# Expert rows that carry gate, token number and residual, answered by a scatter to the output

## The chip, the cores and the metric

The kernel runs on one core of a Trainium2 chip. The metric is the device time of one execution in microseconds (us), the median of several runs. Its engines are PE (TensorE, matrix products), DVE (VectorE), ACT (ScalarE), POOL (GpSimd) and SP (SyncE, which here only issues transfers). They run side by side and meet at semaphores. SBUF is the on-chip memory of 128 partitions, PSUM the accumulator memory of eight banks.

## What is computed

Two layers on four images of 1024 tokens with 64 features. The change touches only the last part, the layer of eight experts with a capacity:

```python
C = max(1, math.ceil(CAPACITY_FACTOR * T / E))          # 1.25 * 4096 / 8 = 640
logits = x @ gate_w + gate_b
probs = jax.nn.softmax(logits, axis=-1)
idx = jnp.argmax(probs, axis=-1)
prb = jnp.take_along_axis(probs, idx[:, None], axis=1)[:, 0]
one_hot = jax.nn.one_hot(idx, E, dtype=jnp.float32)
pos = (jnp.cumsum(one_hot, axis=0) * one_hot).sum(-1).astype(jnp.int32) - 1
kept = pos < C
buf = jnp.zeros((E, C, D)).at[idx, pos_safe].set(x, mode='drop')
hmid = jax.nn.relu(jnp.einsum('ecd,edf->ecf', buf, w1) + b1[:, None, :])
ybuf = jnp.einsum('ecf,efd->ecd', hmid, w2) + b2[:, None, :]
y_tok = ybuf[idx, jnp.minimum(pos, C - 1)] * (prb * kept)[:, None]
y = jnp.nan_to_num(y_tok, nan=0.0, posinf=10000.0, neginf=-10000.0)
out = h + y                                             # x above is layernorm(h)
```

T is 4096 tokens, D is 64, the hidden width is 256. Every token goes to one expert, each expert takes at most 640 tokens, and 8 x 640 = 5120 slots exist for 4096 tokens.

## The kernel before

The program is a row of stages with a barrier of all engines behind each: setup, a loop over the four images (tokens, project, windowed), then experts (first layer), full (second attention), batchnorm and routed. Within a stage each engine has its own list of instructions, in the order in which they are written, and waits only where the code waits on a semaphore. There is no scheduler; what stands in the list of an engine behind a wait is held by it.

The stage routed is the one that changes. Tokens lie as 32 tiles of 128 (ALLT). It runs like this:

- DVE normalises all tokens (L1241 to L1250), PE turns them and forms the gate logits (L1162, L1171), ACT takes the exponential (L1225), DVE picks the expert, PE counts tokens per expert (L1176, L1177), DVE computes the slot of every token and from it two lists of row numbers: `send_to` (L1293) and `fetch_from` (L1299).
- POOL sends each of the 32 tiles with one indirect transfer, 128 rows of 64 floats, to the DRAM buffer `sent_rows` at the rows of `send_to` (L1342). Tokens over the capacity go to spare rows behind the 5120.
- SP waits for all 32 and loads the 5120 rows back in five pieces of 256 KB (L1356). PE turns them in 20 transposes of two tokens side by side, 128 by 128 (L1183), so that one half of the rows of the PE array holds one token's features and the other half the other's. ACT and DVE copy the turned tiles out (L1228, L1305).
- The experts follow one after the other: `hidden` (L1196), two products of 320 columns for each of two halves of the hidden width, one on array rows 0 to 63 and one on rows 64 to 127; ReLU on ACT (L1235) and on DVE (L1318); `outputs` (L1207), five tiles with two products each; the second bias on DVE (L1310). SP stores each expert's answers to the DRAM buffer `answered_rows` (L1360).
- When all eight are stored, POOL gathers for each of the 32 token tiles its 128 answer rows (L1347). For every group of four tiles DVE multiplies by the gate, replaces not-a-number and infinities and adds the residual `res` (L1326 to L1335, eight groups of nine instructions), and SP writes the group to the output (L1363).

`sent_rows` is filled with zeros in the stage batchnorm, by eight transfers on SP (L1088) that SP waits for at the end of that stage.

## Time and profile before

| | |
|---|---|
| median of 3 runs | 1095.16 us (1093.58 to 1095.29) |
| profiled execution: its time | 1091.47 us |
| profiled execution: its span | 1089.6 us |
| stage routed, from its first DVE instruction to the end of the span | 922.5 to 1089.6 us |
| PE, DVE, ACT, POOL busy, share of the span | 68, 57, 41, 34% |
| granted PE clock, mean over the span | 0.837 |

The span is what the trace covers; 1.9 us of the profiled execution's time lie outside of it. Shares of busy time are means over stages with different limits. The change is confined to the last sixth of the span, and there PE, DVE and POOL take turns, which the means don't show.

### The profile page before, as it was taken

The page shows a single profiled execution, that of the slowest core. Times are in us where ns is not written, and L with a number is a line of the kernel's source. Part 1 is how long each engine was busy: PE and PEld are TensorE (multiplying, and loading weights), DVE is VectorE, ACT ScalarE, POOL GpSimd, SP SyncE. Part 2 cuts the span into 40 slices and gives each one's busy share as a digit, 9 for nine tenths or more (in the row PEclk, how much of TensorE's full clock was granted, in tenths as well). Part 3 has the DMA queues.
Part 4 walks back from the last instruction along what each step waited for, and adds up shares of the span by engine and source line. Part 5 has one row for each costly group of instructions (what it writes and reads, how often), then busy time and mean ns, then how long its engine had stood idle before and what let it go on. Part 6 is the DMA issues. An engine that isn't in the chain of part 4 may idle for free. (4 is left out here: it accounts for less than half of the span.)

```text
span 1089.6 us, 21917 instructions
## 1 busy us (share of the span) xinstructions
...
## 2 busy tenths in 40 slices
...
DMA packets 51471, 43.60 MB, mean 40 GB/s; under 512 B 46484, under 2 KB 47956, under 8 KB 50452
## 3 DMA queue, kind: packets, MB, share of 16 engines
...
q0 software_dynamic: 2048, 2.10, 0.8%
q8 instruction: 75, 1.23, 0.5%
q14 instruction: 30, 0.25, 0.1%
...
## 5 line engine op out<-in xcount | busy, mean ns | idle before, releaser
L721 ACT ACTIVATE work<-ps,small,rq 128x160 f32<-128x160 f32 x512 | 243.0, 486 | 51.3 <-DVE small L674 51.1
L700 POOL TENSOR_TENSOR work<-work,small 128x512 f32<-128x512 f32 x128 | 133.1, 1040 | 144.9 <-DVE small L688 144.9
L671 DVE TENSOR_REDUCE ps<-ps 128x4 f32<-128x640 f32 x128 | 106.5, 832 | 60.2 <-PE ps L607 60.2
L682 DVE COPY pT<-ps 128x640 f32<-128x640 f32 x128 | 105.4, 823 | 8.3 <-PE ps L620 7.9
L607 PE MATMUL ps<-kT,big 64*128 64x160 f32 x1024 | 107.1, 333 | 0.0
L721 ACT ACTIVATION_READ_ACCUMULATOR work<-ps,small,rq 128x1 f32 x512 | 104.9, 205 | 0.0
L1342 POOL DMA_INDIRECT sent_rows<-big,xb x32 | 30.8, 964 | 202.2 <-DVEq L1294 192.8
L262 PE MATMUL ps<-xT,s_proj_w 64*128 64x512 f32 x288 | 82.7, 701 | 18.3 <-DVE xb L545 11.7
L572 POOL TENSOR_TENSOR big<-xb 128x1024 f32<-128x1024 f32 x32 | 75.1, 2358 | 55.0 <-DVE xb L545 54.9
L637 PE MATMUL ps<-pT,vwin 128*64 128x128 f32 x1024 | 85.1, 284 | 10.2 <-ACT big L709 2.4
L607 PEld LDWEIGHTS ps<-kT,big 64*128 64x128 f32 x1024 | 83.9, 208 | 0.4
L495 ACT ACTIVATE big<-ps 128x1024 f32<-128x1024 f32 x32 | 32.8, 1023 | 96.3 <-DVE xb L545 96.3
L637 PEld LDWEIGHTS ps<-pT,vwin 128*64 128x64 f32 x1024 | 57.4, 137 | 24.2 <-issue 16.0
L1006 PE MATMUL ps<-xb,big 64*128 64x64 f32 x1024 | 65.2, 277 | 0.9 <-DVE hl L1070 0.9
L1006 PEld LDWEIGHTS ps<-xb,big 64*128 64x128 f32 x1024 | 62.5, 193 | 1.0 <-issue 1.0
L262 PEld LDWEIGHTS ps<-xT,s_proj_w 64*128 64x128 f32 x288 | 30.4, 219 | 64.5 <-issue 38.0
L620 PE MATMUL ps<-s_ident,work 64*128 64x64 f32 x1024 | 56.7, 230 | 2.4 <-DVE pT L682 2.4
L603 PE MATMUL ps<-window_mask,row_of_t 64*128 64x128 bf16 (+1 forms) x256 | 33.1, 254 | 37.0 <-PEq L208 25.0
L634 PE MATMUL ps<-pT,vrem 32*64 32x128 f32 x1024 | 57.7, 295 | 0.0
L709 ACT ACTIVATE big<-ps 128x256 f32<-128x256 f32 x128 | 48.5, 379 | 16.4 <-PE ps L634 16.2
L565 POOL MEMSET vwin<- 128x256 f32 x4 | 1.2, 311 | 159.2 <-POOLq L208 159.2
L1038 ACT ACTIVATE big<-ps,h 128x1024 f32<-128x1024 f32 x32 | 35.6, 1113 | 42.2 <-DVE h L1059 42.2
...
## 6 DMA issues: line engine op xcount, KB each, us to landing
...
```

What stands on the lines that cost most here:

```text
L262: ins = nc.tensor.matmul(bank[banks + w][:], proj_w[half_rows(w), cols], xT[half_rows(w), :], start=True, stop=True)
L572: g.tensor_tensor(dst, first, second, ALU.add).then_inc(S["rot_done"], 1)
L607: ins = nc.tensor.matmul(tiles[e][:, hh, :], qT[half_rows(e), c, 4 * hh:4 * hh + 4, :].rearrange("p a t -> p (a t)"), kT[half_rows(e), CHU ...
L620: ins = nc.tensor.transpose(bank[4 + r][:, D * q:D * q + D], src, ident[half_rows(r), half_rows(r)])
L634: ins = nc.tensor.matmul(o, vrem[r, c, :], pT[r, c % 2, NQ * P:], start=False, stop=True, tile_position=(CHUNK * q, D * e), skip_group_che ...
L637: nc.tensor.matmul(o, vwin[:, c, :], pT[:, c % 2, P * q:P * q + P], start=True, stop=True, skip_group_check=True)
L671: ch.step(v.tensor_reduce(row_max(c), ps[:, s_banks(c), 0:2 * SPAN].rearrange("p e (h k) -> p e h k", h=2), X, ALU.max))
L682: v.tensor_copy(pT[:, c % 2, :].rearrange("p (q r t) -> p r q t", r=2, t=D), ps[:, 4:6, 0:(NQ + 1) * D].rearrange("p r (q t) -> p r q t", ...
L700: g.tensor_tensor(probs[:, c % 3, :, 0:P], probs[:, c % 3, :, 0:P], bc(small[:, c % 4, 3, :], P), ALU.mult)
L709: nc.scalar.activation(oT[:, :, CHUNK * c:CHUNK * (c + 1)].rearrange("p (h a) t -> p h a t", h=2), ps[:, 6:8, 0:P].rearrange("p h (a t) -> ...
L721: nc.scalar.activation(probs[:, c % 3, q, :], bank[2 * (c % 2) + e][:, SPAN * hh:SPAN * hh + SPAN], ACT.Exp, bias=small[:, c % 4, 1, q:q + ...
L1006: ins = nc.tensor.matmul(bank[6 + r][:, 0:D], pT1[half_rows(r), i % 2, P * k:P * k + P], v1[half_rows(r), TILES * (i // TILES) + k, :], st ...
```

## The change

- Each sent row grows from 64 to 130 floats (ROW, 520 bytes): the normalised token, its residual `res`, its gate and its token number as an integer. ACT copies the normalised tokens and the residual into the array `payload` (after's L1234, L1235), DVE writes the other two columns. POOL's sends now also wait for ACT's copies.
- The row of a slot in `sent_rows` is chosen so that the 40 tiles that come back (SLOT_TILES) each hold 128 slots of one expert. `fetch_from`, its four DVE instructions and the array of gates go.
- The empty rows of `sent_rows` are now written in the stage full, from `empty_row`, whose last two floats are 1.0; read as an integer that is a token number far past 4095.
- SP writes `res` to the whole output at the start of routed, one transfer of 1 MB.
- The rows come back in five pieces of 532 KB, eight tiles each. PE turns the five tiles of one expert at a time (`turn_back`, 40 transposes in all), one expert ahead of its products. ACT copies three of the five turned tiles and DVE two (`keep_back`). The turned tiles occupy 64 partitions, so both products of `hidden` use array rows 0 to 63. `hidden` uses two pairs of banks in turn instead of three.
- `answer(e)` on DVE adds the bias and then does the whole end of the computation for one expert's five tiles: gate, replacement of special values, residual. The store to `answered_rows`, the gather and the output transfers of the groups go.
- POOL scatters each of the expert's five tiles straight to the output at the token numbers that came along (40 transfers); row numbers past 4095 are left out by `bounds_check`.

The core of the diff; declarations and unchanged layouts are left out:

```diff
+COPIED_BY_ACT = 3 * P
+GATE_AT, TOKEN_AT, ROW = 2 * D, 2 * D + 1, 2 * D + 2
...
+                v.memset(empty_row[:, 0:TOKEN_AT], 0.0)
+                v.memset(empty_row[:, TOKEN_AT:], 1.0)
...
+            @block.sync
+            def _(sp):
+                for k in range(E):
+                    sp.dma_start(sent_rows[CAPACITY * k:CAPACITY * (k + 1), :].rearrange("(p t) d -> p t d", p=P),
+                                 empty_row[:].unsqueeze(1).to_broadcast([P, CAPACITY // P, ROW])).then_inc(S["zero_done"], 16)
+                sp.wait_ge(S["zero_done"], 16 * E)
...
-                for k in range(E):
-                    sp.dma_start(sent_rows[CAPACITY * k:CAPACITY * (k + 1), :].rearrange("(p t) d -> p t d", p=P),
-                                 zeros[:, 0:D].unsqueeze(1).to_broadcast([P, CAPACITY // P, D])).then_inc(S["zero_done"], 16)
                 sp.wait_ge(S["x_loaded"], 16 * 5)
-                sp.wait_ge(S["zero_done"], 16 * E)
...
         def both(n):
-            return ps[:, 2 * (n % 3):2 * (n % 3) + 2, 0:CAPACITY // 2].rearrange("p a (t s) -> p a t s", s=SLOT_ROWS)
+            return ps[:, 2 * (n % 2):2 * (n % 2) + 2, 0:CAPACITY // 2]
...
-                for t in range(HALF_TILES):
-                    if t % 4 == 0:
-                        pe.wait_ge(S[f"back{t // 4}"], 16)
-                    ins = nc.tensor.transpose(bank[t // 4][:, P * (t % 4):P * (t % 4) + P], came[:, t, :], ident[:])
-                    if t % 4 == 3:
-                        ins.then_inc(S["turned_back"], 1)
+                def turn_back(e):
+                    pe.wait_ge(S[f"back{(PER_EXPERT * e + PER_EXPERT - 1) // 8}"], 16)
+                    if e >= 1:
+                        pe.wait_ge(S["low_done"], e)
+                        pe.wait_ge(S["xT_dve"], e)
+                    for j in range(PER_EXPERT):
+                        b, col = divmod(P * j, COPIED_BY_ACT)
+                        ins = nc.tensor.transpose(bank[4 + b][0:D, col:col + P], came[:, PER_EXPERT * e + j, 0:D], ident[:])
+                    ins.then_inc(S["turned_back"], 1)
 
                 def hidden(n):
-                    e, f = divmod(n, 2)
-                    if n < 3:
-                        pe.wait_ge(S["xT_dve"], (HALF_TILES // 4) // 2)
-                        pe.wait_ge(S["low_done"], HALF_TILES // 4 - (HALF_TILES // 4) // 2)
-                    else:
-                        pe.wait_ge(S["hid_dve" if (n - 3) % 2 else "hid_act"], (n - 3) // 2 + 1)
-                    for a in range(2):
-                        r = slice(D * a, D * a + D)
-                        ins = nc.tensor.matmul(bank[2 * (n % 3) + a][:, 0:CAPACITY // 2], ffn_w[r, P * n:P * n + P],
-                                               came_turned[r, :, SLOT_ROWS * e:SLOT_ROWS * (e + 1)], start=True, stop=True)
+                    e = n // 2
+                    pe.wait_ge(S["low_done"], e + 1)
+                    pe.wait_ge(S["xT_dve"], e + 1)
+                    if n >= 2:
+                        pe.wait_ge(S["hid_dve" if n % 2 else "hid_act"], n // 2)
+                    for w in range(2):
+                        ins = nc.tensor.matmul(bank[2 * (n % 2) + w][:, 0:CAPACITY // 2], ffn_w[0:D, P * n:P * n + P],
+                                               came_turned[:, e % 2, CAPACITY // 2 * w:CAPACITY // 2 * (w + 1)],
+                                               start=True, stop=True)
                     ins.then_inc(S["proj_done"], 1)
 
...
+                turn_back(0)
                 for e in range(E + 1):
+                    if e + 1 < E:
+                        turn_back(e + 1)
                     if e < E:
                         hidden(2 * e)
                         hidden(2 * e + 1)
...
-                for k in range(0, HALF_TILES // 4, 2):
-                    a.wait_ge(S["turned_back"], k + 1)
-                    nc.scalar.activation(came_turned[:, 4 * k:4 * k + 4, :].rearrange("p j n -> p (j n)"), bank[k][:],
+                nc.scalar.activation(xn_sent, xn_all[:], ACT.Copy).then_inc(S["rest_done"], 1)
+                nc.scalar.activation(res_sent, res[:], ACT.Copy).then_inc(S["rest_done"], 1)
+
+                def keep_back(e):
+                    a.wait_ge(S["turned_back"], e + 1)
+                    if e >= 2:
+                        a.wait_ge(S["proj_done"], 2 * (e - 1))
+                    nc.scalar.activation(came_turned[:, e % 2, 0:COPIED_BY_ACT], bank[4][0:D, 0:COPIED_BY_ACT],
                                          ACT.Copy).then_inc(S["low_done"], 1)
...
+                v.tensor_copy(payload[:, :, GATE_AT], sa[3])
+                v.tensor_scalar(payload[:, :, TOKEN_AT].bitcast(I32), spare_rows, float(-E * CAPACITY), None, ALU.add)
...
-                for k in range(1, HALF_TILES // 4, 2):
-                    v.wait_ge(S["turned_back"], k + 1)
-                    v.tensor_copy(came_turned[:, 4 * k:4 * k + 4, :].rearrange("p j n -> p (j n)"),
-                                  bank[k][:]).then_inc(S["xT_dve"], 1)
+
+                def keep_back(e):
+                    v.wait_ge(S["turned_back"], e + 1)
+                    if e >= 2:
+                        v.wait_ge(S["proj_done"], 2 * (e - 1))
+                    v.tensor_copy(came_turned[:, e % 2, COPIED_BY_ACT:], bank[5][0:D, 0:CAPACITY - COPIED_BY_ACT]).then_inc(
+                        S["xT_dve"], 1)
+
+                keep_back(0)
...
                 def answer(e):
+                    tiles = slice(PER_EXPERT * e, PER_EXPERT * e + PER_EXPERT)
+                    by_tile = y_gated.rearrange("p (j d) -> p j d", d=D)
                     v.wait_ge(S["y_psum"], e + 1)
-                    v.tensor_tensor(answers[:, e], bank[6 + e % 2][:, 0:PER_EXPERT * D].rearrange("p (j d) -> p j d", d=D),
-                                    rows(ffn_b2[:, e, :], PER_EXPERT), ALU.add).then_inc(S["y_ready"], 1)
...
-                for gg in range(GROUPS):
-                    v.wait_ge(S[f"got{gg}"], 16 * G)
-                    at = slice(gg * G, gg * G + G)
-                    ch.step(v.tensor_tensor(y_gated.rearrange("p (i d) -> p i d", d=D), fetched[:, at, :],
-                                            bc(gates[:, at], D), ALU.mult))
+                    ins = v.tensor_tensor(by_tile, bank[6 + e % 2][:, 0:PER_EXPERT * D].rearrange("p (j d) -> p j d", d=D),
+                                          rows(ffn_b2[:, e, :], PER_EXPERT), ALU.add)
+                    ch.step(ins)
+                    v.sem_inc(S["y_ready"], 1)
+                    ch.step(v.tensor_tensor(by_tile, by_tile, bc(came[:, tiles, GATE_AT], D), ALU.mult))
                     v.memset(y_finite, 0.0)
                     ch.step(v.tensor_tensor(maski, y_gated, y_gated, ALU.is_equal))
                     ch.step(v.copy_predicated(y_finite, maski, y_gated))
...
-                    v.tensor_tensor(y_out[:, gg, :], y_finite, res[:, at, :].rearrange("p i d -> p (i d)"),
+                    v.tensor_tensor(answers[:, e].rearrange("p (j d) -> p j d", d=D),
+                                    y_finite.rearrange("p (j d) -> p j d", d=D), came[:, tiles, D:2 * D],
                                     ALU.add).then_inc(S["last"], 1)
+
+                for e in range(E):
+                    if e + 1 < E:
+                        keep_back(e + 1)
+                    n = 2 * e + 1
+                    v.wait_ge(S["proj_done"], n + 1)
+                    if e >= 2:
+                        v.wait_ge(S["y_psum"], e - 1)
+                    v.tensor_scalar(hid[:, e % 2, 1].rearrange("p (w n) -> p w n", w=2), both(n), ffn_b1[:, n:n + 1], 0.0,
+                                    ALU.add, ALU.max).then_inc(S["hid_dve"], 1)
+                    if e:
+                        answer(e - 1)
+                answer(E - 1)
...
                 g.wait_ge(S["slots_ready"], 1)
+                g.wait_ge(S["rest_done"], 2)
                 for i in range(ALLT):
                     g.indirect_dma_start(sent_rows, bass.IndirectOffsetOnAxis(send_to[:, i:i + 1].bitcast(U32), 0),
-                                         xn_all[:, i, :], None).then_inc(S["sent"], 16)
-                g.wait_ge(S["slots_ready"], 2)
-                g.wait_ge(S["stored"], 16 * E)
-                for i in range(ALLT):
-                    g.indirect_dma_start(fetched[:, i, :], None, answered_rows,
-                                         bass.IndirectOffsetOnAxis(fetch_from[:, i:i + 1].bitcast(U32), 0)).then_inc(
-                                             S[f"got{i // G}"], 16)
+                                         payload[:, i, :], None).then_inc(S["sent"], 16)
+                g.wait_ge(S["stored"], 16)
+                for e in range(E):
+                    g.wait_ge(S["last"], e + 1)
+                    for j in range(PER_EXPERT):
+                        g.indirect_dma_start(out_rows, bass.IndirectOffsetOnAxis(
+                            came[:, PER_EXPERT * e + j, TOKEN_AT:TOKEN_AT + 1].bitcast(U32), 0),
+                            answers[:, e, D * j:D * j + D], None, bounds_check=IMAGES * SEQ - 1,
+                            oob_is_err=False).then_inc(S["zero_done"], 16)
 
             @block.sync
+                sp.dma_start(out, res[:]).then_inc(S["stored"], 16)
                 sp.wait_ge(S["sent"], 16 * ALLT)
-                back = sent_rows[0:E * CAPACITY, :].rearrange("(p t h) d -> p t (h d)", h=2, t=HALF_TILES)
+                back = sent_rows[0:E * CAPACITY, :].rearrange("(p t) d -> p t d", t=SLOT_TILES)
                 for k in range(CHUNKS_X):
-                    sp.dma_start(came[:, 4 * k:4 * k + 4, :], back[:, 4 * k:4 * k + 4, :]).then_inc(S[f"back{k}"], 16)
-                store = answered_rows.rearrange("(p e j) d -> p e j d", e=E, j=PER_EXPERT)
-                for e in range(E):
-                    sp.wait_ge(S["y_ready"], e + 1)
-                    sp.dma_start(store[:, e], answers[:, e]).then_inc(S["stored"], 16)
-                for gg in range(GROUPS):
-                    sp.wait_ge(S["last"], gg + 1)
-                    sp.dma_start(out[:, gg * G:gg * G + G, :], y_out[:, gg, :].rearrange(
-                        "p (i d) -> p i d", d=D)).then_inc(S["x_loaded"], 16)
-                sp.wait_ge(S["x_loaded"], 16 * GROUPS)
+                    sp.dma_start(came[:, 8 * k:8 * k + 8, :], back[:, 8 * k:8 * k + 8, :]).then_inc(S[f"back{k}"], 16)
+                sp.wait_ge(S["stored"], 16)
+                sp.wait_ge(S["zero_done"], 16 * SLOT_TILES)
```

PE's list for one expert in the middle of the loop, before. `big` is the turned rows or the hidden values, `xb` the weights:

```order
L1196 MATMUL ps<-big,xb 128x320 [waits hid_dve]
L1196 MATMUL ps<-big,xb 128x320
L1196 MATMUL ps<-big,xb 128x320 [waits hid_act]
L1196 MATMUL ps<-big,xb 128x320
L1207 MATMUL ps<-xb,big 128x64 [waits y_ready,hid_dve,hid_act]
L1207 MATMUL ps<-xb,big 128x64 x9
```

The same place in the changed kernel, L1190 being `turn_back`, L1200 `hidden` and L1212 `outputs`:

```order
L1190 MATMUL ps<-s_ident,big 64x128 [waits xT_dve,low_done,back3]
L1190 MATMUL ps<-s_ident,big 64x128 x4
L1200 MATMUL ps<-big,xb 128x320 [waits hid_act,xT_dve,low_done]
L1200 MATMUL ps<-big,xb 128x320
L1200 MATMUL ps<-big,xb 128x320 [waits hid_dve,xT_dve,low_done]
L1200 MATMUL ps<-big,xb 128x320
L1212 MATMUL ps<-xb,big 128x64 [waits y_ready,hid_dve,hid_act]
L1212 MATMUL ps<-xb,big 128x64 x9
```

Five transposes of the next expert's tiles have moved into the loop ahead of each expert's products, with waits on the arriving rows and on the copies of the expert before.

DVE's list, before, at the end of the expert loop and the first group of the gathered rows:

```order
L1318 TENSOR_SCALAR big<-ps,xb 128x2x20x16 [waits y_psum,proj_done]
L1310 TENSOR_TENSOR big<-ps,xb 128x320 [waits y_psum] x2
L1326 TENSOR_TENSOR vwin<-big,xb 128x256 [waits got0]
L1328 MEMSET vwin 128x256 [waits dve_chain]
L1329 TENSOR_TENSOR vwin<-vwin 128x256
L1330 COPY_PREDICATED vwin<-vwin 128x256 [waits dve_chain]
L1331 TENSOR_SCALAR vwin<-vwin 128x256 [waits dve_chain]
L1332 COPY_PREDICATED vwin<-vwin,xb 128x256 [waits dve_chain]
L1333 TENSOR_SCALAR vwin<-vwin 128x256 [waits dve_chain]
L1334 COPY_PREDICATED vwin<-vwin,xb 128x256 [waits dve_chain]
L1335 TENSOR_TENSOR vrem<-vwin,res 128x256 [waits dve_chain]
```

The changed kernel's DVE list for one expert in the middle of the loop: the copy of turned tiles, the ReLU, then `answer`:

```order
L1318 COPY big<-ps 64x256 [waits proj_done,turned_back]
L1350 TENSOR_SCALAR big<-ps,xb 128x640 [waits y_psum,proj_done]
L1327 TENSOR_TENSOR vwin<-ps,xb 128x320 [waits y_psum]
L1331 TENSOR_TENSOR vwin<-vwin,big 128x320 [waits dve_chain]
L1332 MEMSET vwin 128x320 [waits dve_chain]
L1333 TENSOR_TENSOR vwin<-vwin 128x320
L1334 COPY_PREDICATED vwin<-vwin 128x320 [waits dve_chain]
L1335 TENSOR_SCALAR vwin<-vwin 128x320 [waits dve_chain]
L1336 COPY_PREDICATED vwin<-vwin,xb 128x320 [waits dve_chain]
L1337 TENSOR_SCALAR vwin<-vwin 128x320 [waits dve_chain]
L1338 COPY_PREDICATED vwin<-vwin,xb 128x320 [waits dve_chain]
L1339 TENSOR_TENSOR big<-vwin,big 128x320 [waits dve_chain]
```

The nine instructions of a group stood behind the gather; now they stand inside every step of the expert loop, on 320 columns instead of 256.

POOL's list of the stage, before:

```order
L1338 UNCONDITIONAL_BRANCH
L1342 DMA sent_rows<-big,xb 9216x64 [waits slots_ready]
L1342 DMA sent_rows<-big,xb 9216x64 x31
L1347 DMA big<-answered_rows,xb 128x64 [waits stored,slots_ready]
L1347 DMA big<-answered_rows,xb 128x64 x31
```

and its beginning in the changed kernel, where the last two rows come eight times in all:

```order
L1356 UNCONDITIONAL_BRANCH
L1361 DMA sent_rows<-big,xb 9216x130 [waits rest_done,slots_ready]
L1361 DMA sent_rows<-big,xb 9216x130 x31
L1367 DMA out<-big 4096x64 [waits last,stored]
L1367 DMA out<-big 4096x64 x4
```

One wait for all stored answers ahead of 32 gathers has become eight waits, each ahead of five scatters.

## Rows read from the trace of the kernel before

**Rows 1.** Chain that ended last, parts from 957 us: start us, length us, what

```profile
957.69 1.16 POOL sent_rows L1342
...
997.02 2.13 DMA sent_rows<-big,xb
...
1032.17 4.62 PE ps L1207 x40
...
1039.88 0.97 POOL big L1347
...
1080.12 2.77 DMA big<-answered_rows,xb
...
1082.92 0.44 DVE vwin L1326
...
1086.15 0.43 DVE vrem L1335
```

**Rows 2.** Timeline of routed's beginning: start us, length us, engine, line, instruction, idle before

```profile
902.73 1.91 ACT L1110 ACTIVATE big<-hl 128x2048 f32<-128x2048 f32 x1 [15.69 <-DVEq L1118]
...
944.53 0.42 ACT L1225 ACTIVATE xb<-xb 128x256 f32<-128x256 f32 x1 [4.95 <-DVEq L1259]
```

**Rows 3.** Timeline of batchnorm: the filling transfers' issue, and DVE's last instruction

```profile
896.65 7.64 SPq L1088 DMA_DIRECT2D sent_rows<-zeros  x8
...
918.91 2.29 DVE L1129 SCALAR_TENSOR_TENSOR res<-hl,res 128x2048 f32<-128x2048 f32 x1
```

**Rows 4.** Timeline of PE where the rows come back and in the expert loop

```profile
1001.96 1.97 PE L1183 MATMUL ps<-s_ident,big 128*128 128x128 f32 x8 [51.25 <-DMA big<-sent_rows]
...
1004.15 2.82 PE L1183 MATMUL ps<-s_ident,big 128*128 128x128 f32 x12 [0.22 <-DMA big<-sent_rows]
...
1013.84 2.44 PE L1207 MATMUL ps<-xb,big 128*128 128x64 f32 x20
...
1016.21 1.35 PE L1196 MATMUL ps<-big,xb 64*128 64x320 f32 x8
```

**Rows 5.** Timeline of PE's weight loads beside products of 512 columns, full clock

```profile
908.54 0.19 PEld L1103 LDWEIGHTS ps<-big,ones_mean 128*128 128x128 f32 x1 [0.24 <-issue]
908.97 0.19 PEld L1103 LDWEIGHTS ps<-big,ones_mean 128*128 128x128 f32 x1 [0.24 <-issue]
```

**Rows 6.** Stretches: us, busy us (instructions) of PE, PEld, DVE, ACT, POOL, granted clock, DMA share, GB/s

```profile
999.20:1004.20 5.00, 2.01 (x9) 1.61 (x9) 0.23 (x1) 0.60 (x1) 0.00 (x0) 0.50 0.70 242
1007.70:1037.00 29.30, 29.03 (x224) 24.04 (x224) 10.69 (x16) 6.34 (x8) 0.00 (x0) 1.00 0.12 40
1039.90:1081.00 41.10, 0.00 (x0) 0.00 (x0) 23.64 (x63) 0.00 (x0) 31.65 (x32) 0.50 0.23 44
```

**Rows 7.** Groups by line from 1000 us: shapes, count | busy us, mean ns | idle before

```profile
L1318 DVE TENSOR_SCALAR big<-ps,xb 128x640 f32<-128x640 f32 x8 | 7.1, 884 | 7.4 <-PE ps L1196 7.4
...
L1310 DVE TENSOR_TENSOR big<-ps,xb 128x320 f32<-128x320 f32 x8 | 3.9, 491 | 12.1 <-PE ps L1207 12.1
...
L1332 DVE COPY_PREDICATED vwin<-vwin,xb 128x256 f32<-128x256 int32 x8 | 3.6, 445 | 0.3
...
L1228 ACT ACTIVATE big<-ps 128x512 f32<-128x512 f32 x3 | 1.8, 597 | 60.9 <-PE ps L1183 60.9
L1305 DVE COPY big<-ps 128x512 f32<-128x512 f32 x2 | 1.4, 692 | 47.3 <-PE ps L1183 47.3
```

**Rows 8.** The two indirect transfers' POOL instructions: duration ns min/median/max, first and last start

```profile
L1347 POOL DMA_INDIRECT big<-answered_rows,xb x32: 940/944/1192, 1039.9 to 1080.1; - x32
...
L1342 POOL DMA_INDIRECT sent_rows<-big,xb x32: 954/958/1158, 957.7 to 997.0; - x32
```

**Rows 9.** Timeline, POOL's gathers beside one DVE group

```profile
1063.06 1.15 POOL L1347 DMA_INDIRECT big<-answered_rows,xb  x1 [0.30 <-issue]
1063.45 0.29 DVE L1331 TENSOR_SCALAR vwin<-vwin 128x256 int32<-128x256 f32 x1
...
1074.02 0.51 DVE L1331 TENSOR_SCALAR vwin<-vwin 128x256 int32<-128x256 f32 x1
```

76 lines of the change are left out of this document (29 added, 47 removed).

## The prediction

> **What bounds the kernel now.** I read the chain of waits first. From 957.69 us to the end it is one line of work that changes hands: POOL's 32 sends to 997.02, a landing of 2.13, the way back, PE's expert loop up to 1036.8 (the last 40 product records begin at 1032.17), a store, POOL's 32 gathers from 1039.88 to 1080.12, a landing of 2.77, and one DVE group from 1082.92 to 1086.58 [rows 1]. The table of stretches then shows who idles meanwhile: in the expert loop (1007.7 to 1037.0) PE is busy 29.03 of 29.3 us and POOL not at all; in the gathers (1039.9 to 1081.0) POOL is busy 31.65 of 41.1, PE not at all, and DVE 23.64 [rows 6]. So loop and gathers stand one behind the other although they are on different engines. That is what the change touches: the last exchange no longer waits for the last expert.
>
> **Price of one indirect transfer.** Its POOL instruction takes 0.958 us for a send and 0.944 for a gather in the median [rows 8], and the trace shows 0.30 idle between two of them [rows 9]. Start to start the sends come every (997.02 - 957.69)/31 = 1.269 us, the gathers every (1080.12 - 1039.88)/31 = 1.298 [rows 1].
>
> **Ahead of the sends.** The filling of `sent_rows` goes from batchnorm to full. In batchnorm its issue ended at 904.3, DVE worked until 921.2 [rows 3], so removing it gives 0; in full SP does nothing else for some 250 us, so it costs 0 there though it doubles its bytes. ACT gets two copies of 128x2048 behind its exponential, which ends at 944.95; the nearest row, a squaring of the same size, took 1.91, so they end at 948.8 [rows 2]. The sends begin at 957.69 [rows 1]: POOL's new wait is met 9 us early, and without that cover each copy would cost 1.9. DVE's two payload columns (32 elements each) lie in its wait for the counting products: 0. One slot instruction less on the way to `send_to` gives 0.1, two small memsets in setup cost up to 0.2. SP's 1 MB store of `res` is queued ahead of the load of the returning rows, but it is issued at 922 and that load waits until 999: 0. Sum: 0.1 us lost.
>
> **The sends.** 32 as before, but of 520 bytes a row. If POOL's work goes by rows, it stays at 1.269 each; if the wider row had to be described in two parts, it would be up to 0.96 more each. No row shows a second width. I take 0, because send and gather write and read opposite ways and still agree within 0.014 [rows 8], which looks like a price per row; the other end is a rival below. Less than today's price I exclude: there is not less to describe.
>
> **The way back.** The pieces grow from 256 to 532 KB. The first now releases PE at 1001.96, 2.8 us after the load could start, the later ones at 1004.15 [rows 4]; the stretch around it moves 242 GB/s [rows 6]. 0.27 MB more at 240 to 480 GB/s is 0.6 to 1.1 us; I take 0.8 for the first piece (1002.7) and 1.5 more for the second (1004.2).
>
> **PE per expert.** Transposes: (2.82 - 1.97)/4 = 0.21 each [rows 4] at granted clock 0.50 [rows 6], so 0.11 at full clock; five are 0.55, and five at the start at half clock 1.1. `hidden`: at full clock a record of 512 columns takes 0.43 [rows 5], so one of 320 takes 0.27 and eight in a row 2.15. Today the eight take 1.35 [rows 4], because the two halves of the array rows work side by side; in the changed kernel both products use rows 0 to 63 and the whole 2.15 is due. `outputs` stays 2.44 [rows 4]. Together 5.1 us per expert, where it was 3.65.
>
> **DVE per expert.** From 320 columns (491 ns) to 640 (884) a column costs 1.23 ns [rows 7]. The copy of two turned tiles: 0.69 for 512 columns [rows 7], 0.38 for 256. ReLU 0.88. Bias 0.49 [rows 7]. The nine instructions of a group took 3.66 undisturbed [rows 1] on 256 columns, one of the slower of them 445 ns [rows 7]; 64 columns more on eight steps in a row add 0.5 to 0.6: 4.2. With the hand-overs 6.1 us per expert, 4.75 of them from the finished products to the finished answer. ACT has 0.8 for its ReLU and under 0.6 for its copy (0.597 for 512 columns [rows 7]): never late.
>
> **POOL per expert.** Five scatters at 1.245 (0.944 + 0.30) are 6.2 us. Beside DVE they are longer: one gather in four takes about 1.15, each time it lies beside a `TENSOR_SCALAR` from SBUF to SBUF, as at 1063.06 [rows 9]. Until now that happened once per DVE group. In the changed kernel DVE is busy nearly all of the time, with two such instructions, a memset and a copy per expert; I take one to two meetings of 0.21 us: 6.55 per expert, 1.31 per scatter. The Trainium skill (SBUF — State Buffer, section Who interferes with whom) speaks against this change here: it says that GpSimd and a VectorE instruction in a two-port mode exclude each other for the whole instruction. The trace agrees in kind, with 0.2 us per meeting; by the row the sum below stands, by the rule it would be that of the first rival.
>
> **The sum.** POOL (6.55) is slower than DVE (6.1) and PE (5.1), so after the first answer POOL sets the pace. The first answer: turned tiles of expert 0 at 1003.8, copied 1004.3; those of expert 1, whose piece is there, 1005.4; `hidden` of expert 0 on a clock that rises meanwhile (2.15 to 4.3, taken 3.3) 1008.7; transposes 1009.3; `hidden` of expert 1, which stands ahead of `outputs(0)` on PE, 1011.4; `outputs(0)` 1013.8; answer 1018.5. POOL starts its first scatter at 1018.7 and its 40th 39 x 1.31 = 51.1 us later, 1069.8; landing 2.1 as for a send [rows 1], 1071.9; and what now follows the last landing. Today DVE's last instruction ends at 1086.58, the output transfer behind it lands in about 1.9, and the span ends at 1089.6, so 1.1 remain: 1073.0. Against 1089.6 that is 16.6 us less, with the 0.1 above 16.5. The profiled execution took 1091.47, the median of the runs is 1095.16, 3.7 more; I take the gain off the median: **1078.7 us**. In short: 32 gathers, their landing and a group (about 50 us behind the loop) become 40 scatters (51 us), but begin 18 us earlier than the last expert's end.
>
> Bounds of the forecast: scatters undisturbed (1.245) -2.5; first answer 2 earlier or later; `bounds_check`, which no row shows, 0 to 0.2 per scatter (the largest spread of a gather is 0.25 [rows 8]), up to +8; rows that are left out (at least 1024 of 5120) may be cheaper, taken as 0, at best -3. I keep 1074 to 1083 as the forecast's own range.
>
> **Rivals.**
> - **POOL and DVE hold each other up more.** Four meetings per expert of 0.21 make 1.42 per scatter: 39 x 0.11 = +4.3, **1083**. For it: DVE's share rises from 23.64 of 41.1 [rows 6] to nearly all. Against it: DVE itself was held only once, 0.51 instead of 0.29 [rows 9].
> - **Scatter or send dearer, but not doubled** (bounds check, unaligned rows, 0.1 to 0.4 each): +4 to +14, at **1087** in the middle.
> - **Cheaper**, skipped rows cost nothing to describe: **1074**.
> - **Slower: a row of 520 bytes is two pieces of work for POOL.** Then 32 sends cost 0.96 more each, +30.7, nothing hides them (the whole chain stands on them) and the time is **1109**. It decides from 16.5/32 = 0.52 us per send.
> - **PE stays at half clock**, because waits open between the pieces of the loop. Per expert 10.2 instead of 5.1; the first answer at 1024.6, the last at 1096, the span 1104.5, the time **1110**. It decides from 9 us per expert. Against it: the clock is full through today's loop [rows 6] and PE would still be busy 5.1 of 6.5 us.
> - **It doesn't do what it says**: some wait holds the scatters until the last answer, at 1018.5 + 7 x 6.1 = 1061.2. Then 39 x 1.25, 2.1 and 1.1 follow: span 1113, time **1119**. The lists of the engines show no such wait.
>
> **How the numbers follow.** Forecast 0.59, more hold-ups 0.13, dearer 0.12, cheaper 0.04, doubled sends 0.07, half clock 0.03, not as told 0.02. The predicted time is the forecast's. From 1073 to 1090 lie the forecast, the hold-ups and most of the dearer case, a little over 0.8. Within 0.2% (about 2 us, what a measurement of this kernel can tell) of 1095.16 lies only the edge of the dearer case: 0.02. Slower are the last three rivals: 0.12. Faster: 0.86.
>
> **What would show it.** Sends every 1.27 us; `hidden` eight records in about 2.15; DVE from product to answer 4.75; scatters starting near 1018.7, 1.31 apart, with no gaps at the seams between experts; granted clock 1.0 from about 1008 to 1050. Wrong it would be if sends are visibly longer than 1.27, if POOL waits for DVE at every expert (then DVE's 6.1 was too low), or if PE's clock falls back.

## The result: 1.2% slower, and the profile after

The changed kernel took **1110.62 us** (1107.52 to 1112.6, 4 runs) against 1095.22 for the kernel before in the same comparison: 1.012 of it, 95% interval 1.0092 to 1.0148. The forecast was 1078.7, 31.9 less. The profiled execution took 1112.6 and has a span of 1110.8. Two of the kernels further down have executions at two levels, 20 to 30 apart; there both levels are given.

The chain that ended last, of the changed kernel, start and length in us (the counterpart of [rows 1] and [rows 4]):

```profile
962.29 1.15 POOL sent_rows L1361
...
1001.61 2.27 DMA sent_rows<-big,xb
1003.89 4.11 DMA big<-sent_rows
1008.05 1.29 PE ps L1190 x5
...
1011.20 4.56 PE ps L1200 x8
1015.76 1.21 PE ps L1190 x5
1016.96 4.56 PE ps L1200 x8
1021.52 4.46 PE ps L1212 x20
1025.98 1.07 PE ps L1190 x5
1027.05 4.56 PE ps L1200 x8
...
1071.96 4.47 PE ps L1212 x20
```

Behind the way back the chain is TensorE's: 1.07 (transposes), 4.56 (`hidden`), 4.46 (`outputs`), again and again, 10.09 per expert. The same stretches as [rows 6] (us, busy us of PE, PEld, DVE, ACT, POOL, granted clock, DMA share, GB/s):

```profile
962.30:1003.90 41.60, 0.00 (x0) 0.00 (x0) 0.00 (x0) 0.00 (x0) 30.81 (x32) 0.50 0.16 51
1008.00:1077.00 69.00, 68.33 (x217) 49.66 (x218) 31.29 (x66) 9.41 (x15) 24.71 (x24) 0.50 0.09 34
1077.00:1110.80 33.80, 12.70 (x48) 10.61 (x46) 13.34 (x30) 0.79 (x1) 16.25 (x16) 0.50 0.04 11
```

In the second row PE is busy 68.33 of 69.0 us and the clock is still 0.50, 1.2 GHz, all the way; in [rows 6] the old loop has 1.00. POOL, which was to set the pace, waits once per expert. Its sends, its scatters and what ended its waits (durations in ns; then us, times):

```profile
L1361 POOL DMA_INDIRECT sent_rows<-big,xb x32: 954/958/1147, 962.3 to 1001.6; - x32
...
L1367 POOL DMA_INDIRECT out<-big x40: 980/983/1298, 1031.8 to 1102.9; - x40
its engine sat idle before it (us, times) until:
  DVE big L1339: 50.6, 8
  issue: 9.8, 32
```

The sends are what they were [rows 8]. Ahead of the scatters POOL waited eight times, once per expert, for VectorE's answer (L1339); 29.2 of the 50.6 us are the wait for the first one. VectorE itself waits for `outputs`, as here between two experts (timeline, idle time before in brackets):

```profile
1036.11 0.49 DVE L1327 TENSOR_TENSOR vwin<-ps,xb 128x320 f32<-128x320 f32 x1 [3.57 <-PE ps L1212]
...
1036.93 1.16 POOL L1367 DMA_INDIRECT out<-big  x1 [0.30 <-issue]
...
1041.73 0.98 POOL L1367 DMA_INDIRECT out<-big  x1 [3.64 <-DVE big L1339]
```

The end has a surprise. The last scatter starts at 1102.95 and the span ends at 1110.8. In between POOL's sequencer, the part that reads its instruction list, is in an instruction DRAIN at the end of the stage (count: min/median/max ns, first and last start); the first row is of the changed kernel, the second of the kernel before:

```profile
L208 POOLq DRAIN  x17: 34/1499/12039, 0.7 to 1097.8; - x17
```

```profile
L206 POOLq DRAIN  x17: 34/1497/21132, 0.7 to 1065.5; - x17
```

The last one runs from 1097.8 for 12.04, to 1109.8, which is 5.9 after the last scatter instruction's end. SP, which waits for the landing of all scatters, was through by 1105.3, so the landing is not what the end waits for. Before, the drain ended 5.3 after the last gather's end (1065.5 + 21.1 against 1080.1 + 1.19), at 1086.6, and nobody saw it, since the last group and its output ran until 1088.6.

**Where 33 us went.** The two sums below are 33.2 apart, in the profiled execution; the medians are 31.9 apart. I count from the first send, because it began 4.6 later than in the profile of before (962.29 against 957.69). That is no part of the change: the kernel of e5 below has the old code up to there and sent first at 963.2.

| us | first send to first scatter | 40 scatters, first to last start | rest | sum |
|---|---|---|---|---|
| forecast | 61.0 | 51.1 | 3.2 | 115.3 |
| changed kernel | 69.5 | 71.2 | 7.8 | 148.5 |
| before (82.2 to the first gather, 40.2, 9.5) | | | | 131.9 |

### The profile page after: what moved, and what is told of

Read it like the earlier page. It is cut to its first block and busy times, and to the rows that moved or that the text cites. A ratio compares the mean times of both kernels' runs of the same rounds, so it can differ in the third digit from the quotient of the medians.

```text
span 1110.8 us, 22043 instructions
## 1 busy us (share of the span) xinstructions
PE 798.0 (72%) x8626; PEld 534.5 (48%) x8626; DVE 624.6 (56%) x1265; ACT 454.0 (41%) x1369; POOL 377.3 (34%) x428
## 5 line engine op out<-in xcount | busy, mean ns | idle before, releaser
L675 DVE TENSOR_REDUCE ps<-ps 128x4 f32<-128x640 f32 x128 | 106.6, 832 | 61.3 <-PE ps L611 61.3
L264 PE MATMUL ps<-xT,s_proj_w 64*128 64x512 f32 x288 | 85.8, 725 | 17.9 <-DVE xb L549 11.8
L1017 PEld LDWEIGHTS ps<-xb,big 64*128 64x128 f32 x1024 | 64.1, 197 | 1.0 <-issue 1.0
L1367 POOL DMA_INDIRECT out<-big x40 | 41.0, 1024 | 60.4 <-DVE big L1339 50.6
```

What stands on the lines that cost most here:

```text
L264: ins = nc.tensor.matmul(bank[banks + w][:], proj_w[half_rows(w), cols], xT[half_rows(w), :], start=True, stop=True)
L675: ch.step(v.tensor_reduce(row_max(c), ps[:, s_banks(c), 0:2 * SPAN].rearrange("p e (h k) -> p e h k", h=2), X, ALU.max))
L1017: ins = nc.tensor.matmul(bank[6 + r][:, 0:D], pT1[half_rows(r), i % 2, P * k:P * k + P], v1[half_rows(r), TILES * (i // TILES) + k, :], st ...
```

## Experiments

Theory A: the clock stays at half because `hidden`'s two products no longer run side by side on the two halves of the array's rows. Theory B: it was lost at the loop's start, where ten small transposes with waits between them took the place of twenty large ones. Each batch shared its runs of the kernel before (medians of 1095.5 to 1097.0). The kernels ran on five chips.

**e1_before_one_half.** 

> The kernel before, with both products of hidden read from array rows 0 to 63 (the second one too), nothing else changed; half of the slots are then computed from other tokens. Theory A (the clock stays at 1.2 GHz in the changed kernel because its two products of hidden no longer run side by side on the two halves of the array rows): here too the granted clock stays at 0.5 through the expert loop, eight records of hidden take about 4.6 us and twenty of outputs 4.5, the loop grows from 29 to about 73 us and the time by about 43, to 1138. Theory B (the clock is lost at the start of the loop, where the changed kernel has ten small transposes with waits between them in place of twenty large ones): this kernel's start is the old one, so the clock rises at about 1008 us as before; eight records take 2.15, the loop grows by 8 x 0.8 = 6.5 us, the time is about 1102.

The edit went astray: it hit the gate logits (L1171), not `hidden`, so half of the tokens were routed by other tokens' logits, and it tests neither theory. It took 1103.53, 1.0066 (1.0044 to 1.0087). Its one use: the clock, in the old loop, rose only 9 us after PE came back (1013.4 to about 1022) instead of 5, so the time to its rise isn't fixed. The edit meant here was made in e5.

**e2_warm_start**, the changed kernel with the following, and the semaphores changed to suit it

```diff
+                pe.wait_ge(S["sent"], 16 * 29)
+                for k in range(6):
+                    nc.tensor.matmul(bank[0][:], ones[:], big1_flat[:, 0:HALF], start=True, stop=True)
```

> The changed kernel with six extra products of 128x128 by 128x512 on PE, begun when 29 of the 32 sends have landed, so that PE comes busy to the loop (their results are not used). Theory B: the granted clock is 1.0 when the loop begins and stays there; POOL sets the pace; about 1087 us (the 1078.7 forecast, 4.6 for the end of POOL's list after its last scatter, 4 for the other stages). Theory A: the clock may be 1.0 at the start, but falls back to 0.5 within the first experts, and the time stays at 1105 to 1111.

**e3_other_half**, the changed kernel with (shortened)

```diff
                     for w in range(2):
-                        ... ffn_w[0:D, P * n:P * n + P], came_turned[:, e % 2, ...]
+                        ... ffn_w[half_rows(w), P * n:P * n + P], <rows 64 to 127 for w = 1> ...
```

> The changed kernel with the second product of hidden on array rows 64 to 127, where old data lies, so half of the slots get values from those; instructions, shapes and waits are those of the changed kernel. Theory A: the two products run side by side, the granted clock rises to 1.0 early in the loop and stays; eight records of hidden in about 1.35 us, DVE or POOL sets the pace at 6.1 to 6.6 us per expert, time about 1087. Theory B: the clock stays at 0.5; eight records take about half of their 4.56 us, the twenty of outputs 4.46 as now, 7.9 us per expert in place of 10.1: about 1095.

**e4_pairs**, the same idea made whole: two tiles are turned at once, even tiles on rows 0 to 63, odd ones on 64 to 127 (shortened).

```diff
-                for j in range(PER_EXPERT): transpose(bank[4 + b][0:D, ...], came[:, 5 * e + j, 0:D], ident[:])
+                for j in range(4): transpose(bank[4 + k % 2][:, P * j:P * j + P], came[:, 4 * k + j, :], ident[:])
...
+                    for a in range(2):
+                        q, m = pairs_of(e, a)
+                        matmul(bank[2 * (n % 2) + a][:, 0:P * m], ffn_w[half_rows(a), ...], came_turned[half_rows(a), q:q + m, :])
```

> The changed kernel computing the whole layer with half-row products: the normalised halves of the returned rows are loaded first, two tiles side by side, PE turns two tiles at a time with 20 transposes of 128x128, tiles of even number lie on array rows 0 to 63 and those of odd number on 64 to 127; each product of hidden takes an expert's even tiles and its odd tiles side by side (384 and 256 columns). The rest of the returned rows comes in five more loads. Theory A: clock 1.0 from early in the loop, PE about 4.5 us per expert, DVE (5.8) or POOL (6.5) sets the pace, 1083 to 1088 us. Theory B (it is the start): also faster, since the start is again one of large transposes; the two then differ in e2. If neither holds and the clock stays at 0.5: about 1095.

Measured: e2 1086.08, 0.9907 (0.9874 to 0.994); e3 1086.3, 0.9906 (0.9871 to 0.994); e4 1085.55, 0.9886 (0.985 to 0.9922). All three are 24 to 25 us faster than the changed kernel, and all have the clock back. Stretches of e2, e3 and e4 in this order (columns as above):

```profile
1005.20:1055.00 49.80, 45.33 (x265) 35.42 (x263) 39.60 (x87) 10.23 (x16) 26.99 (x25) 0.95 0.12 46
```

```profile
1008.00:1012.00 4.00, 4.00 (x16) 1.94 (x14) 1.30 (x2) 1.28 (x2) 0.00 (x0) 0.50 0.41 170
1012.00:1053.00 41.00, 34.80 (x230) 27.77 (x229) 35.08 (x77) 8.46 (x13) 24.50 (x23) 0.87 0.04 13
```

```profile
1008.60:1012.50 3.90, 3.75 (x13) 1.93 (x12) 0.87 (x2) 1.65 (x4) 0.00 (x0) 0.63 1.38 219
1012.50:1027.00 14.50, 13.01 (x92) 9.76 (x92) 11.06 (x26) 4.71 (x10) 4.21 (x4) 1.00 0.37 62
```

So each cure is enough alone: e2 keeps the serial products and comes to the loop with the clock up; e3 and e4 come at half clock, with no products ahead, and the clock rises within the first products, 7 and 5 us after PE came back. Neither theory alone is it; the changed kernel lacks both.

How soon side-by-side products bring the clock up is another matter. e6 below has them too, and its clock rose only 25 us after PE came back at 1005.0:

```profile
1024.00:1030.00 6.00, 6.00 (x25) 4.41 (x24) 3.49 (x9) 1.54 (x3) 4.49 (x5) 0.50 0.06 15
1030.00:1040.00 10.00, 8.89 (x65) 6.94 (x65) 9.13 (x21) 2.48 (x5) 6.71 (x7) 1.00 0.02 5
```

e13 waited 24 us for it. What decides the delay isn't shown. It cost e6 a first scatter that came 3.7 later than e4's and little more, for the form helps at half clock too: e6's PE took 8.2 per expert there (`outputs` begins at 1013.65, then 1021.82), not 10.1.

**e5_before_hidden_half**, the kernel before with

```diff
-                        r = slice(D * a, D * a + D)
+                        r = slice(0, D)
```

> The kernel before with one edit: both products of its hidden layer (L1195) lie on array rows 0 to 63, so that they stand one behind the other instead of side by side; the second half of the slots is then computed from the other half's tokens, so the output is changed in part. The loop's start, 20 transposes of 128x512, stays. Theory A (TensorE's clock does not rise while the loop consists of half-row products one behind the other, and the changed kernel lost it by that alone): the granted clock is 0.50 over the whole loop of outputs, each record of hidden is about 2.3 apart as at half clock, the loop takes about 70 instead of 29 and the time is 1130 to 1140. Theory B (what decides is the run of small transposes with waits between them at the loop's start, and large products before the loop are enough): the clock rises within 6 to 10 us of the loop's start as it did before, each of the 8 x 8 records of hidden becomes up to 0.14 longer at full clock, the time is 1098 to 1106.

Five executions: 1103.99, 1105.05 and 1108.94 (these three are 1.0094 of before, 1.0058 to 1.0129), and 1134.02 and 1137.71. The profile is of one of the three:

```profile
1008.00:1012.00 4.00, 3.98 (x19) 3.42 (x17) 1.27 (x2) 1.20 (x2) 0.00 (x0) 0.50 0.46 157
1013.00:1045.00 32.00, 31.98 (x182) 24.94 (x183) 9.14 (x13) 5.71 (x8) 0.00 (x0) 1.00 0.08 27
```

With the old start of large transposes the clock rose in front of serial half-row products and stayed up for all of them. So serial half-row products alone don't keep it down. The two long executions lie where theory A put a loop at half clock (1130 to 1140), with a mean granted clock of 0.806 and 0.812 over the span instead of 0.83 to 0.84. No trace of a long one was taken, so where they lost the time is not shown; that the serial form leaves the clock to chance is a guess.

**e16_changed_again and e15_warm_again** ask for that chance: the changed kernel and e2's once more, without an edit.

> The changed kernel itself once more, for the spread of its executions: four of four were at 1107.5 to 1112.6, with the clock at half over the whole loop where it was profiled. Theory F: with nothing that brings the clock up ahead of the loop and serial half-row products in it, it stays at half nearly always; all or nearly all executions lie at 1107 to 1113, and one in which the clock rises by chance would lie at 1085 to 1090. If one of them does, the size of the clock's share in the difference is shown on the unedited kernel.

Five executions, 1111.28 to 1114.68, 1.0156 (1.0131 to 1.018). With the first four that is nine executions, none below 1107; the two that were profiled have the clock at 0.50 through the whole loop.

> The kernel of e2_warm_start once more, for the spread of its executions: four of four were at 1085 to 1089. In e12_all_together, which also keeps half-row products one behind the other and has the same six products ahead of the loop, five of eight executions were 20 longer, at a mean granted clock of 0.81 to 0.82 instead of 0.84 to 0.85. Theory G (a clock that is up is kept by the serial form whatever the loop): again all at 1085 to 1089. Theory F (with serial half-row products it is left to chance): one or more of the 6 to 8 executions at 1105 to 1112.

Twelve executions, 1091.31 to 1097.94, **0.9999** (0.9982 to 1.0016): neither of the expected levels. The clock was up over 1008 to 1036, but TensorE's results came late, and from 1036 on the clock was at half as well (0.51, then 0.50). In the profile ScalarE waited for transposes whose records end at 1038.1 until 1045.8, and TensorE's own products of that time stand apart, "issue" in front of them (waits of ACT, us, times, longest, "remote" being a cause that the trace doesn't name; then timeline):

```profile
ACT big L1245 <- remote: 16.3, 2, 8.6
```

```profile
1036.83 1.25 PE L1194 MATMUL ps<-s_ident,big 128*64 128x128 f32 x5 [1.77 <-DVE big L1322]
...
1044.22 0.98 PE L1216 MATMUL ps<-xb,big 128*128 128x64 f32 x3 [0.20 <-issue]
...
1045.64 2.82 PE L1216 MATMUL ps<-xb,big 128*128 128x64 f32 x12 [0.44 <-issue]
...
1045.81 0.48 ACT L1245 ACTIVATE big<-ps 64x384 f32<-64x384 f32 x1 [8.61 <-remote]
```

POOL waited 12.8 us more between its scatters than in e2. The kernel before, on the same chip, showed nothing of it (1096.72), nor did the changed kernel of e16, whose loop also runs beside scatters: POOL waited 50.4 for answers there and 50.6 in the first trace. Two more kernels ran there and had the same, **e13_pairs_no_meeting** and **e14_pairs_warm** (waits of 15.0 and 13.3, 1099.0 and 1095.14). To tell chip from kernel, e14's and e2's kernels were run again on another one:

> The kernel of e14_pairs_warm once more, on whatever chip comes. There its scatters waited 13.3 in all, of which the records show TensorE's work as late without a cause of the program, and the time was 1095. Theory H (that chip held TensorE up; the forms are not at fault): on another chip the waits are below 2 and the time is 1080 to 1083. Theory K (the kernel does it to itself wherever it runs): 1093 to 1097 again.

> The kernel of e2_warm_start a third time, beside e17_pairs_warm_again on the same chip. It was 0.9907 of the kernel before in the first run and 0.9999 in the second, on two chips, with waits of the scatters of 0.1 and 12.8. Theory H: below 1089 and 0.989 to 0.993 of the kernel before on this chip, 4 to 5 above e17_pairs_warm_again, because its scatters meet VectorE's SBUF steps. Theory K: both levels within one chip, some executions at 1085 to 1089 and some at 1094 to 1098.

e17: 1081.51 (1078.05 to 1082.54), **0.9863** (0.9842 to 0.9884), waits 0.2. e18: 1086.91, 0.9924 (0.9906 to 0.9942), waits 0.1, all six within 1084.89 to 1088.58. Theory H holds as far as it goes: the kernels don't do it to themselves. Whether it was the chip or something at that time, and what held TensorE up, is open.

**Why the scatters are longer than 0.98.** With the clock up, POOL sets the pace, and it is slower than forecast: 54.5 for the run of 40 in e2 and e3. Timeline of e4, POOL beside VectorE:

```profile
1028.80 0.33 DVE L1328 MEMSET vwin<- 128x320 f32 x1
1029.04 0.43 DVE L1329 TENSOR_TENSOR vwin<-vwin 128x320 int32<-128x320 f32 x1
1029.16 1.16 POOL L1364 DMA_INDIRECT out<-big  x1 [0.31 <-issue]
...
1030.06 0.41 DVE L1331 TENSOR_SCALAR vwin<-vwin 128x320 int32<-128x320 f32 x1
1030.50 0.52 DVE L1332 COPY_PREDICATED vwin<-vwin,xb 128x320 f32<-128x320 int32 x1
1030.62 1.23 POOL L1364 DMA_INDIRECT out<-big  x1 [0.30 <-issue]
```

Three of five scatters are 0.18 to 0.25 longer, and VectorE's step is 0.41 once instead of 0.33. The first reading was that each lies beside a step of VectorE that has all its operands in SBUF (`vwin`). Four kernels take these steps away by degrees.

**e6_finite_in_psum** is e4 with the line in the diff below; **e7_best** is e6 with e2's six products, and with `outputs` of expert 0 moved ahead.

> The kernel of e4_pairs with y_finite, the target of the memset and of both TENSOR_SCALARs of VectorE in each expert, moved from SBUF to a PSUM bank; the transposes of rows that come back then share one bank in turn. It computes all. Theory C (GpSimd's scatters, 1.39 apart there against 1.29 in the run of sends, are held up where they lie beside VectorE's memset and its SBUF-to-SBUF operations): the 40 scatters come 1.29 to 1.32 apart, the run of scatters is 3 to 4 shorter, and the time is 1081 to 1082.5. Theory D (the longer scatters have another cause, such as their own data or the traffic of the DMA engines): 1.39 stays, and the time is 1085 to 1087.

> The kernel of e6_finite_in_psum with two more edits: six products of 128x128 by 128x512 on TensorE, whose result nobody reads, from the landing of the 29th send on, so that it comes to the loop of experts with the clock up; and outputs of expert 0 directly behind hidden of expert 1, ahead of the second turn of returned rows. It computes all. If the clock is up at the loop's start, the first scatter begins about 1.5 to 3 earlier than in e4_pairs (1021.9 there), the pace is that of e6_finite_in_psum, and the time is 1077 to 1080 by theory C and 1082 to 1084 by theory D. If both cures of the clock give the same thing, nothing is gained beyond e6_finite_in_psum.

```diff
+        y_finite = bank[5][:, 0:PER_EXPERT * D]
```

**e9_no_finite_steps** is e2 without seven of the steps; **e10_no_sbuf_to_sbuf** is e7 with the second diff.

> The kernel of e2_warm_start without the seven steps of VectorE that turn NaN and infinities of an expert's answer into finite values (memset, is_equal, two TENSOR_SCALARs, three COPY_PREDICATEDs); that part of the computation is left out. VectorE's answer then takes about 1.5 instead of 4.8 per expert, so the first scatter starts about 3 earlier (1017.5 instead of 1020.7). Theory C (the scatters of GpSimd are longer than 0.98 because VectorE's steps lie beside them): 36 to 40 of the 40 scatters take 0.98 to 1.02, they come 1.29 to 1.31 apart, the run of scatters is 50.3 to 51 instead of 54.5, and the time is 1077 to 1079.5. Theory D (the longer scatters come from something else, their own data or the DMA traffic): they still come 1.38 to 1.40 apart, and the time is 1081.5 to 1083.

> The kernel of e7_best, in which y_gated too lies in PSUM, in place in the bank of outputs, and the self comparison that finds NaN (is_equal of two SBUF operands, 0.43 to 0.47, the step beside which the 1.51 scatters of e7_best lie) is one TENSOR_SCALAR that reads PSUM alone (is_ge against minus infinity). It computes all. If the longer scatters are those that meet VectorE steps that only use SBUF (theory C in its narrow form), the 40 scatters now take 0.98 to 1.02 each, the run of 39 spacings is 50.2 to 51 instead of 53.6, and the time is 1082.5 to 1084. If any step of VectorE lengthens them, or another cause does, the sum of the excess over 0.98 stays at 3 to 4 and the time at 1086 to 1088.

```diff
+                    y_gated = bank[6 + e % 2][:, 0:PER_EXPERT * D]
-                    ch.step(v.tensor_tensor(maski, y_gated, y_gated, ALU.is_equal))
+                    ch.step(v.tensor_scalar(maski, y_gated, -float("inf"), None, ALU.is_ge))
```

| kernel | time | of before | sum of what 40 scatters take over 0.98 | first to last start |
|---|---|---|---|---|
| e2 | 1086.08 | 0.9907 | 4.4 | 54.5 |
| e4 | 1085.55 | 0.9886 | 4.0 | 54.1 |
| e6, y_finite in PSUM | 1087.35 | 0.991 (0.9886 to 0.9935) | 3.1 | 54.5, 1.3 of it waits |
| e7, the same and warm | 1086.92 | 0.9915 (0.9895 to 0.9935) | 3.4 | 53.6 |
| e9, steps left out | 1079.22 | 0.9838 (0.9806 to 0.987) | 0.4 | 50.6 |
| e10, y_gated in PSUM too | 1086.37 | 0.9902 (0.9868 to 0.9936) | 0.5 | 50.7 |

Scatters of e10, then of e2 (ns min/median/max): the median is the same, the tail is not.

```profile
L1372 POOL DMA_INDIRECT out<-big x40: 982/983/1302, 1025.7 to 1076.5; - x40
```

```profile
L1371 POOL DMA_INDIRECT out<-big x40: 982/988/1531, 1020.7 to 1075.2; - x40
```

Against theory D: when the steps from SBUF to SBUF are gone, the run is 1.301 per scatter (50.7 over 39), though VectorE is as busy as before. But theory C, in its narrow form too, names the wrong steps. e12 below has no step from SBUF to SBUF either, and six of its scatters still take 1.19 to 1.26, 1.6 in all. Its timeline at one of them:

```profile
1034.81 0.50 DVE L1339 COPY_PREDICATED ps<-vwin,xb 128x320 f32<-128x320 int32 x1
1034.90 1.26 POOL L1367 DMA_INDIRECT out<-big  x1 [0.30 <-issue]
```

What fits all these traces is the VectorE instruction that is under way when the scatter starts. If it reads two operands from SBUF, wherever it writes, the scatter is longer. In e10, e12 and e17 ten scatters start 0.05 to 0.2 after the start of such a COPY_PREDICATED, and these ten take 1.15 to 1.30; the other 110 take 0.98 or 0.99, also those that start inside a TENSOR_SCALAR or TENSOR_TENSOR with an operand in PSUM. The lines of e4 above say the same: its long scatters start 0.12 after a TENSOR_TENSOR `vwin<-vwin` and 0.12 after a COPY_PREDICATED `vwin<-vwin,xb`. The scatters of 1.29 in e6 and e7 meet a COPY_PREDICATED too. Those of 1.51 start inside the MEMSET, 0.19 ahead of the comparison (TENSOR_TENSOR `vwin<-vwin`), which follows the MEMSET without a wait; where the comparison reads PSUM, as in e10, such starts cost nothing. The extra time is what is left of VectorE's instruction, less 0.13: it is 0.53 where the comparison ends 0.66 after the scatter's start (e7), and 0.28 where the COPY_PREDICATED ends 0.41 after it (e12, above). Two scatters that start within 0.04 of such an instruction's start, in e9 and e11, are 0.98 all the same. So e10's run is shorter because the comparison reads PSUM, and because few of its scatters happen to start inside the two COPY_PREDICATEDs per expert that are left; e12 has six that do. This reading was made from the traces afterwards; no run was made to test it.

The Trainium skill (SBUF — State Buffer, section Who interferes with whom) says that a VectorE instruction with two SBUF inputs contends with a GpSimd instruction that reads SBUF, and infers that `tensor_tensor` leaves the writing of a DMA's descriptors alone. By these rows the first holds here, and the inference doesn't: in e2 all six scatters that start inside the TENSOR_TENSOR with two SBUF inputs at L1343 take 1.16 or 1.17 instead of 0.98.

The times of e6, e7 and e10 missed their expectations (1081 to 1082.5, 1077 to 1080 and 1082.5 to 1084 by theory C), in part for another reason, the start. e6's first scatter began 64.1 after the first send, where e4's began after 60.4: that is the clock's late rise. e10's began after 62.8, where e7's began after 61.7, since TensorE waited at 1012 to 1016 and fell back to half clock (0.50 over 1016 to 1020).

**e11_early_first and e12_all_together** tried for the rest.

> The kernel of e10_no_sbuf_to_sbuf, in which the answer of expert 0 is made in two pieces, tiles 0 and 1 and then tiles 2 to 4, so that GpSimd can start after the first. It computes all. GpSimd paces the stage from its first scatter on, so all of what the first scatter gains stays: it starts 1.7 to 2.3 earlier than in e10_no_sbuf_to_sbuf, and the time is 1.7 to 2.3 less, 1080 to 1082 with the contention gone and 1084 to 1086 with it. If instead TensorE or VectorE paced the stage, nothing would be gained.

1087.45, 0.9908 (0.9876 to 0.994), so the expected gain did not come. The first scatter came 2.2 earlier, as said, but POOL then waited 3.3 for experts 1 and 2: with an earlier start it was no longer POOL that set the pace in the first 10 us.

> The kernel of e2_warm_start (tiles of one expert, half-row products, six products ahead of the loop) with three more edits, and all of the reference computed: outputs of expert 0 directly behind hidden of expert 0; ScalarE makes both copies of the turned rows, so that VectorE has none; VectorE's answer works in place in the PSUM bank of outputs, finds NaN with one TENSOR_SCALAR and needs neither y_gated, y_finite nor the memset, so no step of it has all its operands in SBUF. From the traces of e2_warm_start and e10_no_sbuf_to_sbuf: first scatter 20.1 after the last send (22.0 less 1.9), 39 spacings of 1.30, 7.8 from the last scatter's start to the end, together 78.6 after the last send instead of 84.4, so the time is 5 to 6 below e2_warm_start: 1080 to 1081.5. If VectorE (about 6.0 per expert, against 6.5 of GpSimd) or TensorE's clock makes GpSimd wait, 1 to 4 of it are lost: 1082 to 1085.

Eight executions: 1084.9, 1088.54 and 1089.3 (these three are 0.9916 of before, 0.9878 to 0.9954), above the expected 1080 to 1081.5 or, with waits, up to 1085, and five at 1106.9 to 1110.69, with mean clocks of 0.812 to 0.822 against 0.838 to 0.846. The profile is of one of the three, with the clock up from 1008 to the loop's end; none was taken of the five, so their cause is not shown. PE's list has e2's six products, but also 0.9 and 0.5 us of waiting in the first six microseconds of the loop. e2's kernel had no execution above 1098 in 22 on three chips (e2, e15, e18), this one had five in eight: what e2 gained did not carry over safely to a near relative. The first scatter was not earlier either, since VectorE's list has the ReLU of expert 1 ahead of the answer of expert 0.

> The kernel of e4_pairs (returned rows turned two tiles at once, hidden's two products side by side, no products ahead of the loop) with VectorE's answer kept off SBUF-to-SBUF steps as in e10_no_sbuf_to_sbuf. It computes all. In e4_pairs the first scatter began 21.1 after the last send, the 39 spacings were 1.388 and the end came 7.9 after the last scatter's start, 83.1 in all. With spacings of 1.30 it is 79.7, so the time is 3.4 below e4_pairs: 1082. Theory F (side-by-side half-row products bring the clock up, serial ones leave it to chance): none of the executions is 20 above the others. If the clock's rise is chance in every form, some of 6 to 8 executions lie 10 to 25 higher.

> The kernel of e13_pairs_no_meeting with six products of 128x128 by 128x512 on TensorE from the landing of the 29th send on, as in e2_warm_start, so that the loop begins with the clock up. It computes all. In e13 the loop's first 4 to 6 are at half clock (as in e4_pairs, 0.57 over 1008 to 1012), which delays the first scatter by 1 to 2; here that is gone, and GpSimd paces from its first scatter on: 1 to 2 less than e13_pairs_no_meeting, 1080 to 1081.5. If TensorE's first steps are set by the loads and copies instead of its clock, the time is that of e13.

These are e10 with e4's order, without and with the six products. On the chip that held TensorE up they were 1.0017 (0.9996 to 1.0038) and 0.9982 (0.9964 to 0.9999); on the other, e17 is the fastest kernel of the study that computes all, 14 us below before and 29 below the changed kernel. Its stage: 59.9 to the first scatter, 50.7, 7.9. None of the 30 executions of side-by-side kernels on the other chips (e3, e4, e6, e7, e10, e11, e17) lies 7 above the fastest of its kernel; the 24 of e13 and e14 spread over 9 and 7.

**e8_half_scatters**, e2 with `for e in range(E // 2)` around the scatters.

> The kernel of e2_warm_start in which only the 20 scatters of experts 0 to 3 are issued; the tokens of the other experts keep the residual alone. After the last scatter of the changed kernel GpSimd's queue drained for 5.9 before the program went on, with 40 scatters at the end. Theory E (the drain is a fixed cost behind an indirect DMA that has just been issued, or grows with the number of scatters): fixed, there is nothing left of it here, because the queue is idle while experts 4 to 7 are still computed, and the drain at the end of the block is below 1. If the drain is instead paid at the block's end whatever lies between, it is 5 to 6 again. The stage then ends with TensorE's and VectorE's last expert, about 1062, and the time is about 1068 in the first case and 1073 in the second.

1064.54 in one run; neither of the two cases expected (1068 and 1073) came. The last drain started at 1042.3 and took 12.90, so it ended 4.3 after the end of the 20th scatter, at 1055.2, while VectorE worked until 1061.7, and the block ended behind VectorE:

```profile
L208 POOLq DRAIN  x17: 34/1497/12900, 0.7 to 1042.3; - x17
```

So it doesn't vanish, but it can be hidden. It is 4.3 behind 20 scatters, 5.3 behind 32 gathers, 5.9 to 6.0 behind 40 scatters (all kernels with 40). Whether number or kind makes it longer was not separated.

## Why the prediction was wrong, point by point

- **The sends**: right. 1.268 apart at 520 bytes a row, 1.269 at 256. Ahead of them: right, ScalarE's copies ended at 953.3, 9 before the first send.
- **The way back**: 4.1 for the first piece instead of 3.6.
- **PE per expert** is the step that failed. It was worked out at 5.1 "at full clock", with a clock that "rises meanwhile" in the first `hidden`, and the clock didn't rise. Every term doubled: transposes 1.07, `hidden` 4.56, `outputs` 4.46, 10.1 per expert. The reason given against the rival, that the clock is full through today's loop, was taken from a loop that has two things this one has not: a start of large products, and products side by side. e2 and e3 give each back alone, and with either the time falls by 24. The rival "PE stays at half clock" had 0.03 and 1110; its time was right (1110.6), and its price per expert too (10.2 against 10.1). Its cause, "waits open between the pieces of the loop", was not: PE was busy 68.33 of 69.0 us.
- **At full clock** the terms held: in e2 the first scatter came 61.3 after the first send (forecast 61.0), `hidden` took 2.42 (2.15 forecast), transposes 0.71 (0.55), `outputs` 2.44. That the first scatter fits so well is in part luck: the forecast had the clock rise during the first products, and e2 comes with it up. e3, which comes at half clock, has 62.1 and e4 60.4.
- **DVE per expert**: 4.83 from product to answer (1076.45 to 1081.28), forecast 4.75.
- **POOL per scatter**, 1.31: mis-sized. 1.40 in e2, 3.4 over the run. Without VectorE beside it 1.29, not 1.245: a scatter takes 0.983 where a gather took 0.944. The meetings were three per expert instead of one to two, and the widest were 0.5 instead of 0.21. They were also put down to the wrong instruction: the gather of 1063.06 that lies beside a TENSOR_SCALAR [rows 9] starts 0.09 after a COPY_PREDICATED with two SBUF operands, and of instructions with two such operands the new list has six per expert, not the four that were counted.
- **The tail**, "1.1 remain" behind the landing: mis-sized. 3.2 was forecast after the last scatter's start, 7.8 measured, because POOL's drain, hidden in the kernel before, became the last thing of the program: +4.6.
- Put together: 1078.7 + 3.4 + 4.6 + 0.3 = 1087.0, and e2 and e18 measured 1086.08 and 1086.91. The mechanism that the forecast stands on, scatters that begin under the expert loop, is there and is worth 8 to 9 us, not 16.5; with side-by-side products and most of the two-operand meetings gone, 14 (e17). The clock costs the changed kernel 24 and turns it round.
